# Two cross-attention layers on one core: keys, queries and row maxima in two f32r parts on 64-row halves of the array, instead of three bf16 parts on one

## The chip, the cores and the metric

The kernel runs on one core of a Trainium2 chip, written by hand in a low-level language: each engine (TensorE or PE, VectorE or DVE, ScalarE or ACT, GpSimd or POOL, and SyncE or SP, which issues DMAs) gets its own list of instructions, and semaphores join them. The metric is the device time of one execution in microseconds, lower is better.

## The reference

Two layers of cross-attention over 32 batch elements. `x` is [32, 112, 320], the context [32, 375, 512]. There are 20 heads of 16 channels.

```python
q = heads(x @ Wq); k = heads(text @ Wk); v = heads(text @ Wv)       # layer 0: text = 77 rows, ip = the other 298
out = softmax(q k^T / 4) v + softmax(q k_ip^T / 4) v_ip
x = out @ Wo.T + bo + x
# layer 1: text = 371 rows, ip = the last 4
probs_t = softmax(q k_t^T / 4);  text_out = probs_t v_t
qsem = l2norm(probs_t @ text);   sem = qsem @ l2norm(ip)^T
probs_ip = softmax(q k_ip^T / 4 + 0.5 * sem) * spatial_mask
out = (text_out + probs_ip v_ip) @ W_out + b_out + x
```

## The kernel before

**The order.** `stage_order()` (L51 on) writes one list of stages (`o.add(kind, ...)`); every engine walks the same list and takes its part of each stage. So each engine works in order, and PE's order is that of the list. A buffer in PSUM is handed from stage to stage by `o.share`: a stage waits for the signal of the stage that had the buffer as many uses before as there are buffers. The banks `R0` to `R2` (`in_bank`, L56) serve all projections, transposes and the products with the Gram matrix; `ST` (three banks) and `PN` (two banks, `PV` and `NS`) hold scores, maxima and the products with the values.

**One round** (the loop over `b` in `stage_order`) handles one batch element's groups of layer 0 with the keys and queries of the next element among them (`groups0`, `ahead`), then the groups of layer 1 of the element before (`groups1`), then the maxima (`maxima`) of layer 0 of the next element and of layer 1 of this one, with the values, Gram matrix and closing steps in between (`between`).

**Keys and queries.** The projection of plain fp32 weights and context lands in an `R` bank. ACT rounds it to bf16 (`kst[:, 0]`), DVE forms the remainder (`rem`), ACT or DVE rounds that to bf16 (`kst[:, 1]`), POOL forms the third part (`kst[:, 2]`). SP writes the parts to DRAM and reads them back stacked by head: `Ks` [102, 20, 384] holds 16 rows for each of six products of parts, `Qs` [102, 20, 112] the matching ones. A product over 96 rows so gives the score in near fp32.

**Maxima** (`s_max`, L645 to L659 on PE): for each head one matmul, queries as weights, 375 keys as columns: three heads into `ST`, then two into `PN`, eight steps a layer. DVE takes the maximum of each row. The negated maxima are transposed (`m_T`), split into three bf16 parts (ACT, then POOL in `m_split`) and sent by DMA (L1352) as rows 96 on of `Qs`, where rows of ones in `Ks` stand against them.

**Scores** (L666 to L678): a group is four heads; for each of three blocks of 128 keys and each head, one matmul with the keys as weights (102 or 100 rows, 128 columns) and 112 query columns, 12 in a group, into the three banks of `ST`. ACT takes the exponential. `pv0` and `pv1` multiply by the values (L679 to L740, weights of 17 or 21 columns, so four matmuls stand in four column tiles), `y` (L708 to L723) multiplies `pr`, the f32r-rounded probabilities, by the Gram matrix in three results j = 0, 1, 2 with 2, 4 and 6 matmuls, each in an `R` bank that DVE frees (`w<-R,w`, L803).

Of the kernel before, what the change touches and what calls it, by code (L numbers as in the profile page):

```python
# [16 lines left out]
QPART = [0, 1, 2, 0, 1, 0]  # L17
KPART = [0, 0, 0, 1, 1, 2]
CT = [(0, 128), (128, 128), (256, 64)]
HALVES = [(0, 12), (12, 20)]  # L20
# [30 lines left out]
def stage_order():  # L51
# [4 lines left out]
    def in_bank(what, signal, value):  # L56
        o.share("R", 3, what, signal, value)

# [6 lines left out]
    def keys(b, l, m):  # L65
        o.add("k", b, l, m)
        in_bank(("k", b, l, m), "k_rem", o.at("k", b, l, m))
        o.share("rem", 2, ("k", b, l, m), "k_low", o.at("k", b, l, m))

    def queries(b, l):  # L70
        o.add("q", b, l)
        in_bank(("q", b, l), "q_rem", o.at("q", b, l))
# [54 lines left out]
    def maxima(b, l, between):  # L127
        for h in range(0, H, 5):
            for h0, wide in ((h, True), (h + 3, False)):
                o.add("s_max", b, l, h0, wide)  # L130
                if wide:
                    o.share("ST", 1, ("s_max", b, l, h0), "s_max_read", o.at("s_max", b, l, h0, wide))
                else:
                    for part in ("PV", "NS"):
                        o.share(part, 1, ("s_max", b, l, h0), "s_max_read", o.at("s_max", b, l, h0, wide))
                between()
        return m_rows(b, l)

    def m_rows(b, l):
        o.add("m_neg", b, l)  # L140
        yield
        o.add("m_T", b, l)
        in_bank(("m_T", b, l), "m_hi", o.at("m_T", b, l))
        yield
        o.add("m_split", b, l)
# [98 lines left out]
    for m in range(3):  # L244
        in_bank(("image_keys", m), "kip_rem", m + 1)
# [36 lines left out]
    for b in range(B + 1):  # L282
# [92 lines left out]
def xattn_two_layers(nc, a, out):  # L375
# [3 lines left out]
    with ctx:  # L379
# [6 lines left out]
        def sem(name):  # L386
            return ctx.enter_context(nc.semaphore(name))

        kd = [nc.dram_tensor(f"k_split{l}", [B, 3, C, T], bf16, kind="Internal").ap() for l in range(2)]
        qd = [nc.dram_tensor(f"q_split{l}", [B, 3, C, S], bf16, kind="Internal").ap() for l in range(2)]  # L390
# [10 lines left out]
        Ks = [sb(f"Ks{i}", [102, H, KW], bf16) for i in range(2)]  # L401
        Qs = [sb(f"Qs{i}", [102, H, S], bf16) for i in range(2)]
        kst = [sb(f"kst{i}", [128, 3, T], bf16) for i in range(2)]
        rem = [sb(f"rem{i}", [128, T]) for i in range(2)]
        qst = sb("qst", [128, 3, 3, S], bf16)
        qrem = sb("qrem", [128, 3, S])
# [21 lines left out]
        mrem = sb("mrem", [2 * H, S])  # L428
        ms = sb("ms", [2 * H, 3, S], bf16)
# [10 lines left out]
        kip = sb("kip", [128, 3, 3, NI], bf16)  # L440
# [37 lines left out]
        kip_mm, kip_hi, kip_rem, kip_mid, kip_low = (sem(n) for n in ("kip_mm", "kip_hi", "kip_rem", "kip_mid", "kip_low"))  # L478
# [971 lines left out]
```

## Time and profile before

| | |
|---|---|
| median of 3 runs | 2875.29 us (2874.62 to 2877.16) |
| the profiled execution | 2872.28 us, its span 2870.5 us |
| TensorE clock granted | 0.988 of full speed over the span |
| PE, DVE, ACT, POOL busy | 2730.6, 1707.2, 1252.8, 467.4 us |
| DMA | 236.31 MB, 450078 packets |

A row of the timeline is: start in us, length in us, engine, line, instruction, out<-in, shapes (for PE: rows*columns of the weights, then rows x columns that stream), type, count, and in brackets the idle time before it and what ended it. Rows of equal instructions are merged: the length then runs from the first's start to the last's end. A matmul's length holds its way through the array, so the distance between starts tells what one costs in a stream. PEld is the load of weights. An fp32 matmul appears as two passes, one of f32r as one (its type also reads f32).

### The profile page before, as it was taken

How to read it: one execution, taken by the hardware profiler on the slowest of the kernel's cores; microseconds unless marked ns; L12 is line 12 of the kernel's file. 1: busy time of each engine (PE TensorE's matmuls, PEld its weight loads, DVE VectorE, ACT ScalarE, POOL GpSimd, SP SyncE). 2: the span in 40 equal slices, each digit the busy share in tenths (PEclk: the TensorE clock that was granted, in tenths of full speed). 3: DMA queues.
4: the chain of work that ended last, by engine and by line, in shares of the span. 5: the costliest groups of instructions: out<-in, count | busy, mean ns of one | idle time of the engine just before them, and what ended most of it. 6: DMA issues, size and time to landing. Idle time of an engine off the chain costs nothing.

```text
span 2870.5 us, 61414 instructions
## 1 busy us (share of the span) xinstructions
PE 2730.6 (95%) x25096; PEld 2106.1 (73%) x25096; DVE 1707.2 (59%) x3464; ACT 1252.8 (44%) x2265; POOL 467.4 (16%) x681
## 2 busy tenths in 40 slices
PE   6899999999999999999999999999999999999977
PEld 5677777777777777777777777777777777777755
DVE  3465566655566755666655666655666655666644
ACT  2344444444444444444444444444444444444443
POOL 1111111111121111121111111111111111111100
PEclk8999999999999999999999999999999999999988
DMA  7666456765546765546664556664556654557630
GB/s 192 95 83 91 75 81 80 87 83 83 82 77 81 90 83 79 82 75 86 89 85 76 81 77 86 81 94 76 80 78 87 81 92 74 81 81 83 83 34 6
DMA packets 450078, 236.31 MB, mean 82 GB/s; under 512 B 220459, under 2 KB 449787, under 8 KB 449788
## 3 DMA queue, kind: packets, MB, share of 16 engines
q1 hardware_dynamic: 433958, 209.34, 55.0%
q10 hardware_dynamic: 15840, 23.04, 2.7%
q8 instruction: 199, 3.26, 0.6%
q14 instruction: 81, 0.66, 0.1%
HBM read 166.38 MB, written 64.59 MB: 80 GB/s over the span
## 4 chain that ended last, share of the span: by engine, by line
PE 75%; DVE 12%; SPq 4%; DMA 3%; ACT 3%; issue 2%; POOL 0%; DVEq 0%; ACTq 0%; POOLq 0%
PE R L717 7%; PE ST L674 6%; PE R L617 6%; PE R L570 5%; PE PN L691 5%; PE PN L747 5%; PE R L560 4%; PE PN L734 4%; DVE m L901 4%; PE R L566 3%; PE R L720 3%; PE R L722 3%; PE R L631 2%; PE R L632 2%; PE R L768 2%
## 5 line engine op out<-in xcount | busy, mean ns | idle before, releaser
L1135 ACT ACTIVATE p<-ST 128x1344 f32<-128x1344 f32 x320 | 413.0, 1291 | 158.6 <-PE ST L677 157.0
L717 PE MATMUL R<-pr,Gh 128*128 128x448 f32 (+1 forms) x960 | 369.0, 384 | 28.3 <-DVE acc L803 28.3
L806 DVE SCALAR_TENSOR_TENSOR w<-p,pr 128x1344 f32<-128x1344 f32 x160 | 249.3, 1558 | 227.0 <-ACT pr L1150 227.0
L803 DVE TENSOR_TENSOR rem<-R,kst 128x375 f32<-128x375 f32 (+1 forms) x160 | 87.5, 547 | 484.9 <-ACT kst L1030 484.9
L803 DVE TENSOR_TENSOR w<-R,w 128x448 f32<-128x448 f32 (+1 forms) x480 | 290.7, 622 | 105.0 <-PE R L722 96.7
L631 PE MATMUL R<-wvh,ch 128*128 128x320 f32 (+3 forms) x896 | 302.5, 338 | 11.2 <-DVE cl L803 10.9
L632 PE MATMUL R<-wvh,cl 128*128 128x320 f32 (+3 forms) x896 | 279.6, 312 | 0.0
L674 PEld LDWEIGHTS ST<-Qs,Ks 100*128 100x128 bf16 (+1 forms) x3520 | 186.9, 98 | 91.9 <-issue 33.0
L1196 POOL TENSOR_TENSOR kst<-rem,kst 128x375 bf16<-128x375 f32 (+1 forms) x160 | 146.2, 914 | 618.4 <-ACT kst L1030 319.8
L674 PE MATMUL ST<-Qs,Ks 100*128 100x112 bf16 (+1 forms) x3520 | 229.4, 214 | 15.6 <-DMA Qs<-ms 6.7
L1150 ACT ACTIVATE pr<-ST 128x1344 fp32r<-128x1344 f32 x160 | 205.3, 1283 | 81.0 <-PE R L722 81.0
L717 PEld LDWEIGHTS R<-pr,Gh 128*128 128x128 f32 (+1 forms) x960 | 176.5, 184 | 78.6 <-DVE acc L803 39.6
L634 PE MATMUL R<-wvl,ch 128*128 128x320 f32 (+3 forms) x672 | 209.6, 312 | 0.0
L1196 POOL TENSOR_TENSOR cl<-cT,ch 128x476 fp32r<-128x476 f32 x126 | 156.7, 1244 | 297.8 <-ACT ch L1030 297.8
L1030 ACT ACTIVATE V<-R 128x320 f32<-128x320 f32 (+2 forms) x160 | 70.3, 440 | 287.6 <-PE R L635 287.6
L1030 ACT ACTIVATE kst<-R 128x375 bf16<-128x375 f32 (+1 forms) x160 | 77.5, 484 | 253.3 <-PE R L572 138.8
L905 DVE TENSOR_REDUCE m<-ST 112x3 f32<-112x1113 f32 x128 | 167.9, 1312 | 24.3 <-PE ST L658 21.1
L1196 POOL TENSOR_TENSOR qst<-qrem,qst 128x336 bf16<-128x336 f32 x64 | 54.2, 847 | 783.2 <-DVE qst L892 783.2
L1030 ACT ACTIVATE pvt<-PN 128x112 f32<-128x112 f32 (+1 forms) x320 | 97.4, 304 | 187.6 <-PE PN L738 128.9
L720 PE MATMUL R<-pr,Gl 128*115 128x448 f32 (+1 forms) x480 | 176.2, 367 | 0.0
L722 PE MATMUL R<-pr,Gl 128*128 128x448 f32 (+1 forms) x480 | 176.0, 367 | 0.0
L631 PEld LDWEIGHTS R<-wvh,ch 128*128 128x128 f32 (+3 forms) x896 | 162.8, 182 | 17.5 <-issue 11.8
(178 smaller groups left out, 5833.1 us busy)
## 6 DMA issues: line engine op xcount, KB each, us to landing
Ks<-k_split SPq DMA_DIRECT2D x384, 140.6 KB, 6.5
k_split<-kst SPq DMA_DIRECT2D x128, 281.2 KB, 3.0
Ks<-k_split SPq DMA_DIRECT2D x384, 93.8 KB, 9.6
Qs<-q_split SPq DMA_DIRECT2D x384, 70.0 KB, 9.4
cT<-in_ctxT ACTq DMA_DIRECT2D x30, 750.0 KB, 4.7
q_split<-qst SPq DMA_DIRECT2D x128, 84.0 KB, 2.0
k_split<-kst SPq DMA_DIRECT2D x64, 140.6 KB, 2.8
xT<-in_xT SPq DMA_DIRECT2D x32, 192.0 KB, 3.2
```

What stands on the lines that cost most here:

```text
L631: e.matmul(r[0:n, 0:C], h[:, k, 0:n], wh[:, k, :], start=k == 0, stop=False)
L632: e.matmul(r[0:n, 0:C], lo[:, k, 0:n], wh[:, k, :], start=False, stop=False)
L634: e.matmul(r[0:n, 0:C], h[:, k, 0:n], wl[:, k, :], start=False, stop=False)
L674: e.matmul(ST[:, u, S * h:S * h + S], Ks[l][0:m, GH * g + h, 128 * u:128 * u + 128], Qs[l][0:m, GH * g + h, :], start=True, stop=True)
L717: e.matmul(r[0:nj, 0:QW], Gh[0:ROWS[u], q:q + nj], pr[0:ROWS[u], QW * u:QW * u + QW], start=u == 0, stop=False)
L720: e.matmul(r[0:nj, 0:QW], Gl[0:ROWS[u], q:q + nj], pr[0:ROWS[u], QW * u:QW * u + QW], start=False, stop=False)
L722: e.matmul(r[0:nj, 0:QW], Gl[0:nj, GO[j]:GO[j] + nj], pr[0:nj, QW * j:QW * j + QW], start=False, stop=True).then_inc(y_mm, 1)
L803: return e.tensor_tensor(to, x, y, op)
L806: return e.scalar_tensor_tensor(out=to, in0=x, scalar=s, in1=y, op0=op0, op1=op1)
L1030: return e.activation(to, x, ACT.Copy, scale=scale)
L1135: e.activation(p32[i][:].rearrange("p (u q) -> p u q", u=3), st, ACT.Exp).then_inc(p_whole, 1)
L1196: return e.tensor_tensor(to, x, y, ALU.subtract)
```

## The change

1. Keys, queries and negated maxima are kept as two f32r parts (rounded value, and one DVE subtraction). `Ks`, `Qs`, `kst`, `qst`, `ms`, `kip` are f32r; `rem`, `qrem`, `mrem` and the casts and POOL subtractions go. A head takes 3 x 16 rows (high*high, high*low, low*high) instead of 6 x 16.
2. Even heads lie in rows 0 to 47 (plus 4 or 3 rows for maxima), odd heads in rows 64 to 111 (plus the same). Two heads are issued one behind the other, one for each half; the halves write to different banks.
3. `ST` has four banks (`s` = half), the `R` banks are two. The maxima go in seven steps a layer: four, two, four, two, four, two and two heads.
4. The Qs rows of the maxima are sent in 8 (layer 0) and 4 (layer 1) DMAs instead of 6 and 3. Stacks of keys and queries keep six DMAs each.
5. The last four matmuls of each `pv` signal instead of the last one; ACT waits for both halves; `ORDER` maps heads to their places in p.

```diff
-QPART = [0, 1, 2, 0, 1, 0]
-KPART = [0, 0, 0, 1, 1, 2]
+QPART = [0, 0, 1]
+KPART = [0, 1, 0]
+KR, HALF = 3 * D, 64
+HP = H // 2
+ORDER = [0, 2, 1, 3]
+MAX_STEPS = [(0, 2, True), (2, 1, False), (3, 2, True), (5, 1, False), (6, 2, True), (8, 1, False), (9, 1, True)]
...
-        o.share("R", 3, what, signal, value)
+        o.share("R", 2, what, signal, value)
...
-        in_bank(("k", b, l, m), "k_rem", o.at("k", b, l, m))
-        o.share("rem", 2, ("k", b, l, m), "k_low", o.at("k", b, l, m))
+        in_bank(("k", b, l, m), "k_low", o.at("k", b, l, m))
...
-        Ks = [sb(f"Ks{i}", [102, H, KW], bf16) for i in range(2)]
-        Qs = [sb(f"Qs{i}", [102, H, S], bf16) for i in range(2)]
+        Ks = [sb(f"Ks{i}", [128, HP, KW], f32r) for i in range(2)]
+        Qs = [sb(f"Qs{i}", [128, HP, S], f32r) for i in range(2)]
...
-        ST = pb("ST", [128, 3, 512])
+        ST = pb("ST", [128, 4, 512])
...
-        R = [pb(f"R{i}", [128, 512]) for i in range(3)]
+        R = [pb(f"R{i}", [128, 512]) for i in range(2)]
...
+        def head_rows(x, pair, n, half):
+            return x[HALF * half:HALF * half + n, pair]
...
                 elif kind == "s_max":
...
-                    for u in range(n - 1):
-                        e.matmul(to[0:S, u, 0:T], Qs[l][0:96, h0 + u, :], Ks[l][0:96, h0 + u, 0:T], start=True, stop=True)
+                    for j in range(n):
+                        for half in range(2):
+                            to = ST[0:S, 2 * half + j, 0:T + 1] if wide else PN[0:S, half, 0:T + 1]
+                            mm = e.matmul(to, head_rows(Qs[l], p0 + j, KR, half), head_rows(Ks[l], p0 + j, KR, half)[:, 0:T + 1],
+                                          start=True, stop=True)
...
                 elif kind == "scores":
...
-                        for h in range(GH):
-                            if u < 2 or h < GH - 1:
-                                e.matmul(ST[:, u, S * h:S * h + S], Ks[l][0:m, GH * g + h, 128 * u:128 * u + 128],
-                                         Qs[l][0:m, GH * g + h, :], start=True, stop=True)
+                        for j in range(2):
+                            for half in range(2):
+                                to = ST[:, 2 * half + u // 2, 256 * (u % 2) + S * j:256 * (u % 2) + S * j + S]
+                                mm = e.matmul(to, head_rows(Ks[l], 2 * g + j, m, half)[:, 128 * u:128 * u + 128],
+                                              head_rows(Qs[l], 2 * g + j, m, half), start=True, stop=True)
...
                 elif kind == "k":
...
-                    tt(rm[:, 0:n], r[:, 0:n], s[:, 0, 0:n], ALU.subtract).then_inc(k_rem, 1)
-                    if j % 2:
-                        w.wait_ge(k_rem, j + 1)
-                        e.tensor_copy(s[:, 1, 0:n], rm[:, 0:n]).then_inc(k_mid, 1)
+                    tt(s[:, 1, 0:n], r[:, 0:n], s[:, 0, 0:n].bitcast(fp32), ALU.subtract).then_inc(k_low, 1)
...
+                elif kind == "m_T":
...
+                    tt(ms[0:n, 1, :], R[slot["R", ("m_T", b, l)]][0:n, 0:S], ms[0:n, 0, :].bitcast(fp32),
+                       ALU.subtract).then_inc(m_low, 1)
...
+                elif kind == "m_out":
...
-                        for u in range(3):
-                            r0 = 96 + 3 * c + u
-                            e.dma_start(Qs[l][r0:r0 + 1, :, :], ms[H * c:H * c + H, u, :]).then_inc(d_m[l], 16)
+                        for half in range(2):
+                            r0, h0 = HALF * half + KR + 2 * c, H * c + HP * half
+                            for u in range(2):
+                                e.dma_start(Qs[l][r0 + u:r0 + u + 1].bitcast(fp32),
+                                            ms[h0:h0 + HP, u, :].bitcast(fp32)).then_inc(d_m[l], 16)
```

How PE's order changes in the stretch of the maxima, around the product with the image values (`vbd`) and the second block of the Gram matrix (`cT`), before:

```order
L656 MATMUL ST<-Ks,Qs 112x375 [waits s_max_read]
L656 MATMUL ST<-Ks,Qs 112x375
L658 MATMUL ST<-Ks,Qs 112x375
L797 MATMUL R<-vbd,prT 112x320 [waits vbd_made,ip_T_copied,g_lo]
L656 MATMUL PN<-Ks,Qs 112x375 [waits s_max_read]
L658 MATMUL PN<-Ks,Qs 112x375
L642 MATMUL R<-cT 128x247 x3
L643 MATMUL R<-cT 128x247
```

and after:

```order
L656 MATMUL PN<-Ks,Qs 112x376 [waits s_max_read]
L656 MATMUL PN<-Ks,Qs 112x376
L793 MATMUL R<-vbd,prT 112x320 [waits vbd_made,ip_T_copied]
L656 MATMUL ST<-Ks,Qs 112x376 [waits s_max_read]
L656 MATMUL ST<-Ks,Qs 112x376
L644 MATMUL R<-cT 128x247 [waits v_copied]
L644 MATMUL R<-cT 128x247 x2
L645 MATMUL R<-cT 128x247
```

The maxima steps still stand singly between full-height stages; a step is one or two pairs, and each matmul has 48 rows in one half.

On PE, the first group of `y` in a round (`Gh`, `Gl` are the parts of the Gram matrix; `pvT_read` is DVE's reading of the transposed products with the values, `w_times_y` its reading of a `y` result), before:

```order
L674 MATMUL ST<-Qs,Ks 128x112 [waits p_round]
L674 MATMUL ST<-Qs,Ks 128x112 x10
L677 MATMUL ST<-Qs,Ks 128x112
L717 MATMUL R<-pr,Gh 128x448 [waits v_copied]
L722 MATMUL R<-pr,Gl 128x448
L717 MATMUL R<-pr,Gh 128x448 [waits v_copied]
L720 MATMUL R<-pr,Gl 128x448
L717 MATMUL R<-pr,Gh 128x448
L722 MATMUL R<-pr,Gl 128x448
L717 MATMUL R<-pr,Gh 115x448 [waits pvT_read]
```

and after:

```order
L676 MATMUL ST<-Qs,Ks 128x112 [waits p_round]
L676 MATMUL ST<-Qs,Ks 128x112 x11
L716 MATMUL R<-pr,Gh 128x448 [waits v_copied]
L721 MATMUL R<-pr,Gl 128x448
L716 MATMUL R<-pr,Gh 128x448 [waits pvT_read]
L719 MATMUL R<-pr,Gl 128x448
L716 MATMUL R<-pr,Gh 128x448
L721 MATMUL R<-pr,Gl 128x448
L716 MATMUL R<-pr,Gh 115x448 [waits w_times_y]
```

The wait for `pvT_read` moved from the third result to the second, and the third now waits for the reader of the first.

On SP, around the rows of the maxima, before:

```order
L1308 DMA xn<-in_x 112x320
L1363 DMA out<-x_1 112x320
L1352 DMA Qs<-ms 1x20x112 x6
L1303 DMA xT<-in_xT 128x3x128
L1317 DMA k_split<-kst 128x3x375
L1352 DMA Qs<-ms 1x20x112 x3
```

and after:

```order
L1280 DMA xn<-in_x 112x320
L1340 DMA out<-x_1 112x320
L1328 DMA Qs<-ms 1x10x112 x8
L1275 DMA xT<-in_xT 128x3x128
L1289 DMA k_split<-kst 128x2x375
L1328 DMA Qs<-ms 1x10x112 x4
```

The place of the rows in SP's queue stays, behind the store of an output; there are more of them, with half the heads each.

## Rows read from the trace of the kernel before

**Rows 1.** The page: busy time by engine, and the chain by engine.
```profile
PE 2730.6 (95%) x25096; PEld 2106.1 (73%) x25096; DVE 1707.2 (59%) x3464; ACT 1252.8 (44%) x2265; POOL 467.4 (16%) x681
...
PE 75%; DVE 12%; SPq 4%; DMA 3%; ACT 3%; issue 2%; POOL 0%; DVEq 0%; ACTq 0%; POOLq 0%
```

**Rows 2.** Windows of one round: stretch, length, busy us of each engine.
```profile
1497.50:1523.30 25.80, 24.25 (x139) 19.32 (x138) 23.74 (x56) 9.99 (x28) 6.79 (x8) 1.00 0.50 84
1523.30:1549.30 26.00, 25.91 (x311) 19.78 (x311) 7.41 (x16) 12.11 (x21) 5.87 (x10) 1.00 0.19 53
1549.30:1584.50 35.20, 34.26 (x339) 26.01 (x334) 22.24 (x39) 16.98 (x25) 1.93 (x3) 1.00 0.90 98
sum 87.00, PE 84.41 PEld 65.11 DVE 53.39 ACT 39.08 POOL 14.59; mean PE 28.14 PEld 21.70 DVE 17.80 ACT 13.03 POOL 4.86
```

**Rows 3.** Waits of PE, the longest: us in total, times, longest.
```profile
PE R L717 <- DVE acc L803: 28.3, 30, 0.9
```

**Rows 4.** The chain in order of time, in the maxima.
```profile
1519.35 3.99 DMA Qs<-ms
```

**Rows 5.** Timeline of the maxima: DVE, SP's queue, the next scores.
```profile
1512.39 1.32 DVE L905 TENSOR_REDUCE m<-ST 112x3 f32<-112x1113 f32 x1
...
1515.12 0.32 SPq L1363 DMA_DIRECT2D out<-x  x1
...
1515.49 4.58 SPq L1352 DMA_DIRECT2D Qs<-ms  x6
...
1523.39 0.71 PE L674 MATMUL ST<-Qs,Ks 102*128 102x112 bf16 x11 [0.28 <-DMA Qs<-ms]
```

**Rows 6.** Timeline of PE: a scores group and what follows.
```profile
1527.00 0.71 PE L674 MATMUL ST<-Qs,Ks 102*128 102x112 bf16 x11
...
1527.60 1.12 PE L566 MATMUL R<-cT,wk 128*128 128x128 f32 x8
```

**Rows 7.** Timeline of PE: a step of the maxima.
```profile
1507.84 0.30 PE L635 MATMUL R<-wvl,ch 128*128 128x320 f32 x1
1507.98 0.48 PE L656 MATMUL ST<-Ks,Qs 96*112 96x375 bf16 x2
...
1508.46 0.70 PE L797 MATMUL R<-vbd,prT 80*112 80x320 f32 x2
```

**Rows 8.** Timeline of PE: f32r value matmuls behind a step of the maxima.
```profile
1506.08 0.45 PE L631 MATMUL R<-wvh,ch 128*128 128x320 f32 x1
1506.36 0.32 PE L632 MATMUL R<-wvh,cl 128*128 128x320 f32 x1
```

**Rows 9.** Timeline of PE in narrow windows: the query projection's passes.
```profile
1541.68 0.28 PE L617 MATMUL R<-xT,wq 128*128 128x128 f32 x1
...
1541.89 0.37 PE L617 MATMUL R<-xT,wq 64*128 64x128 f32 x1
...
1542.10 0.27 PE L617 MATMUL R<-xT,wq 64*128 64x128 f32 x1
...
1542.30 0.38 PE L617 MATMUL R<-xT,wq 128*128 128x128 f32 x1
...
1542.52 0.39 PE L617 MATMUL R<-xT,wq 128*128 128x128 f32 x2
...
1542.74 0.28 PE L617 MATMUL R<-xT,wq 128*128 128x128 f32 x1
```

**Rows 10.** Timeline of PE, narrow window: values, four column tiles.
```profile
1544.62 0.28 PE L691 MATMUL PN<-p,V 128*17 128x112 f32 x4
```

**Rows 11.** Timeline of the first and last y group of a round.
```profile
1554.75 0.37 PE L717 MATMUL R<-pr,Gh 128*128 128x448 f32 x1
...
1556.67 0.46 PE L717 MATMUL R<-pr,Gh 128*115 128x448 f32 x1 [0.94 <-DVE acc L803]
...
1580.66 0.36 PE L717 MATMUL R<-pr,Gh 128*115 128x448 f32 x1
1580.77 1.16 DVE L803 TENSOR_TENSOR w<-R,w 128x448 f32<-128x448 f32 x2
```

More of the change, by code:

```diff
@@ L127, in maxima @@
     def maxima(b, l, between):
[L128 to L136, printed above, removed]
+        for p0, n, wide in MAX_STEPS:
+            o.add("s_max", b, l, p0, n, wide)
+            for part in ("ST",) if wide else ("PV", "NS"):
+                o.share(part, 1, ("s_max", b, l, p0), "s_max_read", o.at("s_max", b, l, p0, n, wide))
+            between()
         return m_rows(b, l)
@@ L387, in sem @@
             return ctx.enter_context(nc.semaphore(name))
-        kd = [nc.dram_tensor(f"k_split{l}", [B, 3, C, T], bf16, kind="Internal").ap() for l in range(2)]
-        qd = [nc.dram_tensor(f"q_split{l}", [B, 3, C, S], bf16, kind="Internal").ap() for l in range(2)]
+        kd = [nc.dram_tensor(f"k_split{l}", [B, 2, C, T], fp32, kind="Internal").ap() for l in range(2)]
+        qd = [nc.dram_tensor(f"q_split{l}", [B, 2, C, S], fp32, kind="Internal").ap() for l in range(2)]
+        rowsd = [nc.dram_tensor(f"rows{i}", shape, fp32, kind="Internal").ap()
+                 for i, shape in enumerate(([4, HP, KW], [3, HP, KW], [1, HP, S]))]
         vipd = nc.dram_tensor("v_ip", [B * NIP, C], fp32, kind="Internal").ap()
@@ L400, in xattn_two_layers @@
         wo = [sb(f"wo{i}", [128, 3, C]) for i in range(2)]
-        Ks = [sb(f"Ks{i}", [102, H, KW], bf16) for i in range(2)]
-        Qs = [sb(f"Qs{i}", [102, H, S], bf16) for i in range(2)]
[L403 to L406, printed above, removed]
+        Ks = [sb(f"Ks{i}", [128, HP, KW], f32r) for i in range(2)]
+        Qs = [sb(f"Qs{i}", [128, HP, S], f32r) for i in range(2)]
+        kst = [sb(f"kst{i}", [128, 2, T], f32r) for i in range(2)]
+        qst = sb("qst", [128, 3, 2, S], f32r)
         V0t = sb("V0t", [TEXT0, H, FV0])
@@ L427, in xattn_two_layers @@
         mn = sb("mn", [S, 2 * H])
-        mrem = sb("mrem", [2 * H, S])
-        ms = sb("ms", [2 * H, 3, S], bf16)
+        ms = sb("ms", [2 * H, 2, S], f32r)
         sip = [sb(f"sip{i}", [S, H, NIP]) for i in range(2)]
@@ L439, in xattn_two_layers @@
         vbd = sb("vbd", [H * NIP, C])
-        kip = sb("kip", [128, 3, 3, NI], bf16)
+        kip = sb("kip", [128, 3, 2, NI], f32r)
         ninv = sb("ninv", [128, B, NIP])
@@ L539, in v_place, with by_pair @@
             return (V0 if l == 0 else V1)[0:n, t], n
-        k_odd = {}
-        for key, j in nk.items():
-            k_odd[key] = sum(1 for i in nk.values() if i <= j and i % 2 == j % 2)
+        def head_rows(x, pair, n, half):
+            return x[HALF * half:HALF * half + n, pair]
+        def by_pair(x):
+            return x.rearrange("p (j s) n -> p s j n", s=2)
         def tensor(e):
@@ L782, in tensor @@
                     w.wait_ge(ns_read, b + 1)
[L783 to L784 removed]
+                    for h, i in enumerate(ORDER[:-1]):
+                        e.transpose(r[0:S, 96 * h:96 * h + 96], nss[:, S * i:S * i + S], ident[0:96, 0:96])
                     e.transpose(r[0:S, 288:384], nss[:, 336:448], ident[0:96, 0:96]).then_inc(ns_T, 1)
@@ L1325, in sync @@
                         w.wait_ge(s_mm, s_nth[b - 1, l, 2 if part == 0 else 4])
-                    for g in range(6):
-                        e.dma_start(Ks[l][D * g:D * g + D, h0:h1, 0:T],
-                                    kd[l][b, KPART[g], D * h0:D * h1, :].rearrange("(h d) t -> d h t", d=D)).then_inc(
-                                        d_kr[l][part], 16)
+                    for half in range(2):
+                        for i in range(3):
+                            r0 = HALF * half + D * i
+                            heads = kd[l][b, KPART[i]].rearrange("(j s d) t -> s d j t", s=2, d=D)[half, :, h0:h1, :]
+                            e.dma_start(Ks[l][r0:r0 + D, h0:h1, 0:T].bitcast(fp32), heads).then_inc(d_kr[l][part], 16)
                 elif kind == "q":
```

237 lines of the change are left out of this document (102 added, 135 removed).

## The prediction

> **What bounds the kernel now.** I read the page first: the matrix engine's share and the chain that ended last [rows 1]. PE is busy 95% of the span and carries 75% of the chain, so PE's stream of matmuls is the bound and everything else matters where PE waits for it. Then the busy time of each engine in the three stretches of one round (one batch element) [rows 2]: the stretch of the maxima (25.8 us) has PE 24.25 and DVE 23.74 us busy, the stretch of layer 0's groups (26.0 us) has PE 25.91 and DVE 7.41, the stretch of layer 1's groups (35.2 us) PE 34.26 and DVE 22.24. A round is 87 us and there are 32. So outside the maxima only PE's own time counts; in the maxima two engines are nearly full. Third, the list of waits: the longest of PE's, for DVE before a y group, is 28.3 us in all [rows 3]. What the change removes from DVE, ACT and POOL in the key and query chains (the remainders, casts and second subtractions) therefore buys next to nothing: it lies beside a PE that does not wait for it. Fourth, the chain in the stretch of the maxima: its last piece is not PE but the DMA of the maxima rows, 3.99 us [rows 4], and before it the six issues of that DMA on SP, 4.58 us, which start at 1515.49 behind an output store [rows 5]. The next scores start at 1523.39, after 0.28 us of waiting for that DMA.
>
> **Scores, 12 matmuls a group, 320 groups.** Today 12 bf16 matmuls take 0.60 us (1527.00 to 1527.60), 50 ns each, and the first matmul behind them starts 0.05 us after the last: weights of 128 columns load unseen and nothing drains [rows 6]. After the change each group is 6 pairs, one matmul in each 64-row half. No row shows f32r with 112 columns, nor two row halves at once; these are the unknown prices.
> Streaming: ten f32r matmuls of 320 columns take 1.48 us (1506.36 to 1507.84 [rows 7, 8]), 148 ns each or 0.46 ns a column: 52 ns for 112 columns.
> Switch of row mode: the query projection alternates 128-row and 64-row matmuls. Steady 128-row passes are 0.11 us apart (1542.52 to 1542.74, two); across a switch the distance is 0.21 and 0.20, so about 0.095 us of draining each way; and the pass behind the switch is followed after 0.21 or 0.22 instead of 0.11 [rows 9]: the load of 128 four-byte columns, about 0.105 us, is no longer hidden. By the page TensorE: Matmul & The Clock Gate of the Trainium skill (sections LDWEIGHTS and Weight-path perf modes), a load costs its columns, not its rows, and the fast load is for dtypes narrower than fp32 only; by that rule halving the rows saves nothing and the step from bf16 to f32r makes each load dearer, and the trace agrees (hidden at 50 ns in [rows 6], 105 ns bare in [rows 9]).
> Are the two halves concurrent? The nearest row is four fp32 matmuls in four column tiles that together take 0.28 us [rows 10], where a single pass has a length of 0.27 [rows 9]; so tiles run beside each other, and I take it for row halves. The page TensorEngine Tiling (Array Packing) of the Trainium skill (Tiling Modes, Key Properties) says that different tiles can load and multiply in parallel; by that rule a pair costs what one matmul with its load costs, as forecast, and no row here shows it for row halves. The same section says that a change of tiling mode drains the array; with it the time is the forecast's too, and without it rival D's.
> A pair then costs the larger of 52 ns (stream) and about 108 ns (load, both halves loading together). I take the load, since it is the nearest row; bounds are 52 ns (load hidden) and 214 ns (the two loads one after the other; short f32r streaming no faster than the two passes of plain fp32, 2 x 0.11 x 112/128 = 0.19 us, lies between these). A group: first load 0.105, five distances of 0.108, last stream 0.052, drain 0.095: 0.79 us against 0.60, so +0.19. Behind it the next stage's load is bare, 0.105, where today it costs between nothing and 0.13 (0.28 instead of 0.148 behind a bf16 stage [rows 8]); I take +0.03. In front, five of ten groups now follow a stage without a mode of its own (keys, values, a transpose, a projection), +0.095 for half of them, +0.05. Sum +0.28 us a group, 320 groups: +90 us. With 52 ns a pair it is -0.05 a group, -16 us; with 214 ns +0.91, +291 us.
>
> **Maxima, 40 heads a round.** Today 0.16 us a head (3 in 0.48 [rows 7]). After: 20 pairs of 376 columns, 376 x 0.46 = 174 ns, the load of 112 columns hidden under it: 3.5 us instead of 6.4. But each of 14 steps is now a mode of its own in the middle of 128-row stages: drain 0.095, bare load 0.09, drain 0.095, bare load behind 0.03 more than today: 0.31 a step, about 13 separate steps, 4.0 us. PE's time rises by 1.1 us a round. The price of the halves failing to run together is 20 x 174 ns more, 3.5 us.
> What ends the stretch is the chain of the maxima rows. The m rows of layer 0 go out in eight DMAs instead of six: at 4.58/6 = 0.76 us each [rows 5] that is +1.5 us. The rounding parts now come one subtraction after the copy instead of three POOL steps, but SP stands at the output store until 1515.12 anyway, so that gain is hidden; and the store waits for a DVE addition that now stands behind a four-head reduction, 1.32/3 = 0.44 us longer [rows 5]. So +1.9 us if the issue price holds for smaller transfers (10 source rows instead of 20), and if that price halves, 8 x 0.38 = 3.05 us, the chain is shorter and PE's 1.1 us less its present idle time (25.80 - 24.25) decides: about 0. I take +1.5, nearer to the row as it stands: 31 rounds, +46 us.
>
> **Banks.** Scores take four banks, so the other results have two instead of three. A stage now waits for the reader of the stage two before. I looked where that reader is late. First y group of a round: its second result (1554.75) must now wait for the same reader, acc, that today the third waits for (1556.67, after 0.94 of waiting): the second's four matmuls, 4 x 0.205 us, are no longer in front of the wait, +0.8 us. Last y group: the third result started at 1580.66, and the reader of the first ends about 1580.77 + 0.58 = 1581.35: +0.7 us [rows 11]. Elsewhere the reader is done or so nearly (the three middle groups, where longer scores in front give DVE more room). +1.5 us a round, 32 rounds: +48 us. Bounds: 0.7 (only one of the two) and 3 us (all results of the y groups late by as much again), 22 to 96 us.
>
> **Sum.** 2872.28 us for the profiled execution (span 2870.5) + 90 + 46 + 48 = 3056 us; the median of the runs is 2875.29, 3 us more, which I add in part: 3058 us, 6.4% slower.
>
> **Rivals.**
> A: the two halves' loads go one after the other (or short f32r streams slower): pair 190 to 214 ns. For it: nothing shows parallel loads of rows. Against: the four tiles of [rows 10] start together. Scores cost +240 to +290 instead of +90: 3210 to 3260 us.
> B: the halves do not run together at all. Scores as in A, maxima 3.5 us more a round, +110: about 3370 us. Against it is [rows 10].
> C: loads are fully hidden, the drains stay: scores -16, the rest as forecast: 2950 us.
> D, on the other side of before: f32r halves load hidden under each other and no drain separates them from the 128-row stages. A group is then 6 x 52 = 0.31 us instead of 0.60, -0.29, 320 groups: -93 us. The maxima cannot give much, since DVE is busy 23.74 of 25.8 us and the chain runs through it: about -0.5 us a round, -15; banks +22. 2786 us. The mechanism decides from the point where a switch costs less than 0.05 us; [rows 9] show 0.2 for each, twice in a row, with plain fp32, which is what speaks against it. What speaks for it: the matrix engine is the bound, and the change halves the number of streams there.
> E: all cancels, within 0.2% (about 6 us, what a measurement here can tell from no change).
>
> **Chances.** Forecast with its own bounds (2990 to 3130) 0.51; A 0.17; B 0.05; C 0.11; D 0.14; E 0.02. Faster by over 0.2%: 0.14; within: 0.02; slower: 0.84. The range takes in C and A and leaves out D and B: 2890 to 3270.
>
> **What would show it.** In the profile after: in a scores group, pairs that start together (within some 10 ns) and are about 108 ns apart; 52 would be C or D, 190 or more A, and starts evenly spaced without pairs B. A distance of about 0.2 us from the last matmul before a maxima step to its first, and again behind it; 0.05 would be D. 14 stretches of maxima with PE about 7.5 us in a round against 6.4. PE waiting before a y group's second result, for acc, and in the last y group before its third, for w. SP's issues of the maxima rows: eight, 6.1 us, and scores of layer 0 waiting for that DMA by more than 0.28 us. DVE, ACT and POOL less busy without an effect on the span. The forecast is wrong if the mode switch costs PE nothing, or if the loads of the two halves queue up.

## The result and the profile after

The changed kernel takes 3131.66 us (median of 4 runs, 3120.56 to 3135.34) against 2876.22 us (4 runs, 2874.62 to 2878.33) of the kernel before on the same chip: ratio 1.0881, 95% interval 1.0853 to 1.0910, 255 us slower. The forecast was 3058 us, the range 2890 to 3270. The profiled execution is the longest of the four: 3135.34 us, its span 3133.5 us. The mean granted TensorE clock fell from 0.988 to 0.960.

The page of the kernel after: busy time by engine, granted clock in 40 slices, shares of the chain.

```profile
PE 2940.5 (94%) x25096; PEld 2135.2 (68%) x25096; DVE 1619.3 (52%) x3250; ACT 1214.7 (39%) x2121; POOL 202.2 (6%) x265
...
PEclk8999999999999999999999999999999999999988
...
PE 67%; DVE 14%; SPq 7%; issue 4%; ACT 4%; DMA 4%; DVEq 0%; POOL 0%; ACTq 0%; POOLq 0%
```

Against [rows 1]: PE has as many instructions and is busy 210 us longer, DVE, ACT and POOL are busy 88, 38 and 265 us less, and the span does not gain by it. The other 53 us of the span's 263 are time in which PE stands. On the chain PE's share fell by 8 points, and SP's queue rose from 4 to 7%.

Windows of one round of the kernel after, cut at the first maxima, the first scores of layer 0 and the first scores of layer 1; columns as in [rows 2], the number behind POOL is the granted clock.

```profile
1630.30:1659.60 29.30, 26.93 (x142) 18.82 (x141) 23.62 (x55) 10.59 (x27) 4.96 (x4) 0.94 0.22 47
1659.60:1686.85 27.25, 27.22 (x311) 20.57 (x311) 5.55 (x13) 10.88 (x16) 0.39 (x3) 1.00 0.24 74
1686.85:1726.25 39.40, 37.37 (x336) 27.22 (x331) 21.02 (x34) 16.28 (x24) 0.98 (x2) 0.96 0.78 112
```

The middle stretch has the full clock, and PE does not wait in it: 27.25 against 25.95 us for five scores groups. The other two contain something that [rows 2] do not: a clock below 1.00.

One round is a sample of one. So I cut the traces at the same three places in the 23 to 28 rounds between 300 and 2700 us (mid-run, below). Us of each stretch, the median, and the shortest in brackets where a fall of the clock makes it differ:

| kernel | maxima | layer 0 | layer 1 | sum of the medians |
|---|---|---|---|---|
| before | 25.91 | 25.95 | 34.70 | 86.6 |
| after | 28.99 (27.31) | 27.25 | 39.43 (37.89) | 95.7 |
| b_two_banks | 26.03 | 25.95 | 37.34 | 89.3 |
| b_reordered | 25.90 | 25.95 | 33.94 | 85.8 |
| b_two_banks_reordered | 26.01 | 25.95 | 36.97 | 88.9 |
| a_first_move | 27.50 | 27.25 | 37.37 | 92.1 |
| a_bf16_halves | 28.05 (26.99) | 25.21 | 37.01 | 90.3 |
| a_one_half | 29.04 | 30.58 | 42.09 (40.56) | 101.7 |
| a_reordered | 30.03 (28.37) | 27.25 | 37.36 | 94.6 |

The list of waits, PE's longest, kernel after (us in all, times, longest):

```profile
PE R L716 <- DVE acc L799: 42.1, 30, 1.4
PE R L786 <- DVE fus L799: 40.9, 31, 4.1
PE ST L676 <- DMA Qs<-ms: 27.2, 32, 5.4
PE R L716 <- DVE w L799: 20.3, 33, 0.6
```

Before, acc had 28.3 us [rows 3], fus 19.7 and the maxima rows 6.7, and w was not in the list. The timeline of the kernel after: PE at a step of the maxima, SP's queue at the maxima rows, and the first two scores groups on PE (of the second first its first two matmuls alone, from a narrow window, then all twelve):

```profile
1633.47 0.31 PE L637 MATMUL R<-wvl,ch 128*128 128x320 f32 x1
1633.70 0.60 PE L656 MATMUL ST<-Ks,Qs 48*112 48x376 f32 x4
1634.23 0.58 PE L644 MATMUL R<-cT 128*128 128x375 f32 x1
...
1651.04 6.84 SPq L1328 DMA_DIRECT2D Qs<-ms  x8
...
1659.63 0.88 PE L676 MATMUL ST<-Qs,Ks 52*128 52x112 f32 x12 [0.92 <-DMA Qs<-ms]
...
1663.55 0.32 PE L676 MATMUL ST<-Qs,Ks 52*128 52x112 f32 x2
...
1663.55 0.88 PE L676 MATMUL ST<-Qs,Ks 52*128 52x112 f32 x12
1664.36 0.49 PE L568 MATMUL R<-cT,wk 128*128 128x128 f32 x2
```

In the second group the first two matmuls together take 0.32 us, hardly more than a single one (0.28 on the mean): they start at once, the halves are a pair. In 85% of all pairs the partners start 0 to 4 ns apart, and pairs stand 110 ns apart; the group takes 0.81 us to the next matmul (forecast 0.79) against 0.60 [rows 6]. A step of the maxima starts 0.23 us behind the last value matmul, which alone would be 0.148: the switch of row mode is paid. The issues of the eight DMAs take 6.84 us on SP in this round, which is one of the longest; the median of 24 rounds in mid-run is 6.13 us, 0.77 each (0.76 was expected). The scores wait 0.92 us for these DMAs here and 0.67 in the median, against 0.03 in the median before.

What the forecast does not have, kernel after, two falls of the granted clock: windows of 3.4 us before and behind the point, twice (columns as above).

```profile
1594.60:1598.00 3.40, 2.49 (x22) 1.86 (x21) 2.59 (x4) 2.56 (x3) 0.00 (x0) 1.00 1.12 128
1598.00:1601.40 3.40, 2.91 (x8) 2.52 (x9) 1.79 (x5) 0.00 (x0) 0.00 (x0) 0.61 1.14 132
1635.90:1639.30 3.40, 2.19 (x11) 0.94 (x9) 3.30 (x10) 2.02 (x8) 1.27 (x1) 1.00 0.00 0
1639.30:1642.70 3.40, 3.40 (x16) 3.06 (x14) 2.26 (x3) 0.42 (x2) 1.21 (x1) 0.56 0.00 0
```

And the same two places in the timeline of PE:

```profile
1596.73 0.36 PE L721 MATMUL R<-pr,Gl 128*128 128x448 f32 x1
1598.49 0.56 PE L716 MATMUL R<-pr,Gh 128*128 128x448 f32 x1 [1.40 <-DVE acc L799]
1598.86 0.57 PE L719 MATMUL R<-pr,Gl 128*128 128x448 f32 x1
...
1638.59 0.26 PE L786 MATMUL R<-ident_sb,fus 112*80 112x112 f32 x1 [1.21 <-DVE fus L799]
...
1639.97 0.47 PE L633 MATMUL R<-wvh,ch 128*128 128x320 f32 x1
1640.24 0.47 PE L634 MATMUL R<-wvh,cl 128*128 128x320 f32 x1
```

Behind an idle time of 1.40 us, matmuls of 448 columns are 0.37 us apart instead of 0.205, behind one of 1.21 us those of 320 columns 0.27 instead of 0.148. The granted clock is then at the lower of its two levels, 1.2 instead of 2.4 GHz, for about 3.4 us. Rounds with such a stretch take 1.5 us (layer 1) and 1.6 us (maxima) more in the median than rounds without. In the trace of before it is there for 70.6 us in 7 pieces, all at the start and the end; in the trace after for 250.0 us in 53 pieces, 44 of them (160 us) in the middle. Before has no idle time of PE above 0.95 us in mid-run.

### The profile page after: what moved, and what is told of

The parts are those of the page before. It is cut to its first block, busy times and chain, and to the rows that moved or that the text cites. A ratio compares the mean times of both kernels' runs of the same rounds, so it can differ in the third digit from the quotient of the medians.

```text
span 3133.5 us, 61223 instructions
## 1 busy us (share of the span) xinstructions
PE 2940.5 (94%) x25096; PEld 2135.2 (68%) x25096; DVE 1619.3 (52%) x3250; ACT 1214.7 (39%) x2121; POOL 202.2 (6%) x265
## 4 chain that ended last, share of the span: by engine, by line
PE 67%; DVE 14%; SPq 7%; issue 4%; ACT 4%; DMA 4%; DVEq 0%; POOL 0%; ACTq 0%; POOLq 0%
PE ST L676 8%; PE R L716 7%; PE R L619 5%; SPq L1328 5%; PE PN L692 5%; PE R L572 4%; PE R L562 4%; DVE m L886 3%; PE PN L743 3%; PE R L719 3%; DVE w L802 3%; PE R L568 3%; PE PN L733 3%; DMA Qs<-ms 3%; PE R L721 3%
## 5 line engine op out<-in xcount | busy, mean ns | idle before, releaser
L716 PE MATMUL R<-pr,Gh 128*128 128x448 f32 (+1 forms) x960 | 405.5, 422 | 62.4 <-DVE acc L799 42.1
L799 DVE TENSOR_TENSOR kst<-R,kst 128x375 fp32r<-128x375 f32 (+1 forms) x160 | 87.6, 548 | 504.2 <-ACT kst L1022 504.2
L676 PEld LDWEIGHTS ST<-Qs,Ks 52*128 52x128 f32 (+1 forms) x3840 | 248.7, 190 | 124.2 <-issue 55.0
L676 PE MATMUL ST<-Qs,Ks 52*128 52x112 f32 (+1 forms) x3840 | 291.9, 282 | 33.7 <-DMA Qs<-ms 27.2
L716 PEld LDWEIGHTS R<-pr,Gh 128*128 128x128 f32 (+1 forms) x960 | 186.9, 195 | 164.3 <-DVE acc L799 53.3
L890 DVE TENSOR_REDUCE m<-ST 112x4 f32<-112x1484 f32 (+1 forms) x128 | 192.5, 1504 | 10.8 <-PE ST L656 6.7
L719 PE MATMUL R<-pr,Gl 128*115 128x448 f32 (+1 forms) x480 | 188.6, 393 | 0.0
L1022 ACT ACTIVATE kst<-R 128x375 fp32r<-128x375 f32 (+1 forms) x160 | 77.2, 482 | 284.0 <-PE R L574 156.1
L634 PEld LDWEIGHTS R<-wvh,cl 128*128 128x128 f32 (+3 forms) x896 | 171.1, 191 | 0.3
L572 PE MATMUL R<-cT,wk 128*128 128x298 f32 x576 | 162.1, 418 | 0.0
```

The costliest lines, as they stand in the source:

```text
L572: e.matmul(r[:, TEXT0:T], wk[1][:, k, c0:c0 + 128], c[:, k, TEXT0:T], start=k == 0, stop=False, skip_group_check=True)
L634: e.matmul(r[0:n, 0:C], lo[:, k, 0:n], wh[:, k, :], start=False, stop=False)
L676: mm = e.matmul(to, head_rows(Ks[l], 2 * g + j, m, half)[:, 128 * u:128 * u + 128], head_rows(Qs[l], 2 * g + j, m, half), start=True, stop ...
L716: e.matmul(r[0:nj, 0:QW], Gh[0:ROWS[u], q:q + nj], pr[0:ROWS[u], QW * u:QW * u + QW], start=u == 0, stop=False)
L719: e.matmul(r[0:nj, 0:QW], Gl[0:ROWS[u], q:q + nj], pr[0:ROWS[u], QW * u:QW * u + QW], start=False, stop=False)
L799: return e.tensor_tensor(to, x, y, op)
```

## The experiments

Names with b_ are edits of the kernel before, with a_ of the kernel after. Ratios are against the kernel before, run beside it on the same chip.

| kernel | median us | ratio (95%) | clock | at half clock, us (pieces) |
|---|---|---|---|---|
| b_two_banks | 2979.61 | 1.0361 (1.0344 to 1.0378) | 0.981 | 112.7 (20) |
| b_max_64rows | 2946.82 | 1.0248 (1.0233 to 1.0264) | 0.987 | 77.3 (8) |
| b_scores_64rows | 2918.29 | 1.0155 (1.0136 to 1.0174) | 0.985 | 88.4 (7) |
| a_bf16_halves | 2974.90 | 1.0346 (1.0330 to 1.0362) | 0.978 | 134.4 (29) |
| a_one_half | 3346.95 | 1.1640 (1.1611 to 1.1669) | 0.972 | 187.1 (28) |
| a_stream_56 | 3127.56 | 1.0882 (1.0853 to 1.0911) | 0.956 | 276.6 (56) |
| a_reordered | 3125.73 | 1.0871 (1.0846 to 1.0896) | 0.966 | 212.0 (32) |
| a_bf16_reordered | 3015.17 | 1.0488 (1.0467 to 1.0509) | 0.974 | 159.4 (32) |
| a_first_move | 3049.89 | 1.0608 (1.0584 to 1.0631) | 0.982 | 113.4 (12) |
| b_reordered | 2853.71 | 0.9924 (0.9904 to 0.9944) | 0.987 | 74.3 (8) |
| b_two_banks_reordered | 2945.43 | 1.0248 (1.0229 to 1.0268) | 0.989 | 68.1 (7) |
| b_reordered_ip_later | 2855.95 | 0.9938 (0.9917 to 0.9959) | 0.988 | 69.9 (8) |

### Do the two halves run together? a_one_half

The odd heads' matmuls read the even heads' rows (rows 0 to 47), so the odd heads are left out of the maxima and the scores.

```diff
-            return x[HALF * half:HALF * half + n, pair]
+            return x[0:n, pair]
```

> The changed kernel with both heads of a pair read from the lower 64 rows (so the even head is computed twice, the odd one left out): same instructions, but no two halves at once. Theory that halves run together: each scores pair goes from 0.11 to about 0.22 us (two loads one behind the other in one half), +0.65 us a group, 320 groups +208 us; maxima 20 x 0.174 us more a round, of which idle time hides up to 1, +80 to +108 us: about 3420 us. Rival (the halves never ran together, the pair distance is issue alone): within 20 us of 3131.

3346.95 us, 215 more than after and 73 less than expected. A scores group of this kernel, timeline of PE:

```profile
1605.16 1.54 PE L676 MATMUL ST<-Qs,Ks 51*128 51x112 f32 x12
1606.63 0.47 PE L716 MATMUL R<-pr,Gh 128*128 128x448 f32 x1
```

1.47 us instead of 0.81: the 12 start one after the other, 0.11 us apart in the median, as far as pairs do in the kernel after. Layer 0 with its five groups takes 3.33 us more, 0.67 a group, as expected. The maxima take only 1.4 us more (29.04 against 27.60 in rounds of the kernel after without a fall), where about 3 were expected. Forecast and rival B are told apart: in the kernel after, the halves load and multiply beside each other, and where they are kept from it the time comes near to rival B's 3370. That is what the page TensorEngine Tiling (Array Packing) of the Trainium skill (Key Properties) says of different tiles, and the trace agrees for row halves with the 110 ns a pair.

### What bounds a pair, the load or the stream? a_stream_56 and a_bf16_halves

a_stream_56: each scores matmul streams 56 of its 112 query columns; the other half of the scores is left out (`ST` is set to zero once, at the start).

```diff
-  to = ST[:, 2 * half + u // 2, 256 * (u % 2) + S * j:256 * (u % 2) + S * j + S]
+  to = ST[:, 2 * half + u // 2, 256 * (u % 2) + S * j:256 * (u % 2) + S * j + S // 2]
-                head_rows(Qs[l], 2 * g + j, m, half), start=True, stop=True)
+                head_rows(Qs[l], 2 * g + j, m, half)[:, 0:S // 2], start=True, stop=True)
```

> The changed kernel, but each scores matmul streams only the first 56 of 112 query columns (the other half of the scores is left out). Theory that a pair is bound by the load of its weights, 128 f32r columns, 0.11 us: pairs stay 0.11 us apart, only the last stream of a group is shorter by 0.03 us, 320 groups -8 us: about 3123 us. Rival that f32r streams few columns slowly (0.11 us for 112): pairs at 0.06 us, -0.27 us a group, about 3045 us.

a_bf16_halves: the same layout in bf16. Keys, queries and maxima then hold two parts of bf16, 16 bits where the kernel before has three parts and 24.

```diff
-        Ks = [sb(f"Ks{i}", [128, HP, KW], f32r) for i in range(2)]
-        Qs = [sb(f"Qs{i}", [128, HP, S], f32r) for i in range(2)]
+        Ks = [sb(f"Ks{i}", [128, HP, KW], bf16) for i in range(2)]
+        Qs = [sb(f"Qs{i}", [128, HP, S], bf16) for i in range(2)]
...
```

> The changed kernel with its two parts in bf16 instead of f32r (layout, halves, banks and order kept; the parts hold fewer bits). Theory that f32r loads of 128 columns at 0.11 us set the pairs: a pair falls from 0.11 to about 0.05 us, a scores group from 0.81 to about 0.42, 320 groups -122 us, and 0.07 us less a maxima step, -30: about 2980 us, if the waits and clock falls stay. Rival that draining and pairing are the price: hardly under 3080 us, with pairs still about 0.1 us apart.

Half the stream: 3127.56 us, 4 less than after, the intervals on top of each other. Half the width of the loaded type: 2974.90 us, 157 less. The groups of the two, timeline of PE, first with 56 columns, then in bf16:

```profile
1603.54 0.85 PE L676 MATMUL ST<-Qs,Ks 51*128 51x56 f32 x12
1604.33 0.48 PE L716 MATMUL R<-pr,Gh 128*128 128x448 f32 x1
```

```profile
1607.54 0.47 PE L676 MATMUL ST<-Qs,Ks 51*128 51x112 bf16 x12
1608.00 0.47 PE L716 MATMUL R<-pr,Gh 128*128 128x448 f32 x1
```

0.79 us with half the columns, 0.46 in bf16 with all of them (0.40 in the median of all groups, pairs 0.05 us apart), 0.81 after. So the stream does not set the pair and the width of the type does: that fits the load of 128 four-byte columns, as forecast from [rows 9]. A floor of 0.11 us for a pair of f32r matmuls, whatever they load, would fit as well; no run varies the columns of the weights. The rule in the page TensorE: Matmul & The Clock Gate of the Trainium skill (Weight-path perf modes), no fast load for fp32, agrees, if f32r counts as fp32 there, which the page does not say. The bf16 group is also shorter than the 0.60 us of before [rows 6]: 64-row halves do pay where the load is hidden, and in layer 0 as a whole, drains included, they save 0.74 us (25.21 against 25.95). What is left of a_bf16_halves above before, 100 us, is maxima, banks and clock.

### What does a switch of row mode cost? b_scores_64rows and b_max_64rows

In the kernel before the scores' matmuls (first edit) or those of the maxima (second edit) read 64 rows; the terms in the other rows are left out. The count of matmuls, their columns and the banks stay; only the row mode (128 rows of the array or 64) changes.

```diff
-                    m = 102 if l == 0 else 100
+                    m = 64
```

```diff
-  e.matmul(to[0:S, u, 0:T], Qs[l][0:96, h0 + u, :], Ks[l][0:96, h0 + u, 0:T], start=True, stop=True)
+  e.matmul(to[0:S, u, 0:T], Qs[l][0:64, h0 + u, :], Ks[l][0:64, h0 + u, 0:T], start=True, stop=True)
```

> The kernel before, but the scores' bf16 matmuls read 64 rows of 102 or 100 (they leave out two products of parts and the maxima). My step: draining behind each of 320 groups 0.095 us plus 0.03 of bare load, and 0.095 in front of half of them: 0.17 to 0.19 us a group, +55 to +62 us, about 2935 us. Rival (changes of mode are cheap): within 10 us of before.

> The kernel before, but the maxima's bf16 matmuls read 64 of the 96 rows (they leave out two of the six products of parts), so each of their steps is a change of row mode. My step: 0.095 us of draining in, 0.095 out, and the next load bare: about 0.24 us for each of 12.6 separate steps, 3.1 us of PE a round, of which DVE and the maxima rows' DMA hide about 0.5: about +80 us, 2955 us. Rival (the change of mode costs little and the f32r loads are the price): under +20 us.

+44 us for 320 groups, 0.14 us each. The group itself keeps its length (eleven matmuls in 0.71 us, as in [rows 6]), timeline of PE:

```profile
1507.10 0.71 PE L674 MATMUL ST<-Qs,Ks 64*128 64x112 bf16 x11
...
1507.66 0.21 PE L677 MATMUL ST<-Qs,Ks 64*128 64x112 bf16 x1
```

It is the entry and the exit that cost: from the first matmul of a group to the first one behind it the median over all groups is 0.69 us against 0.59 before, so 0.10 for the exit. For the maxima +72 us, 2.0 us a round in the stretch of the maxima (27.92 against 25.91), with 16 steps. So the price exists, rival D (no drain) is excluded, and it is somewhat below what [rows 9] gave: 44 us where 55 to 62 were expected, 72 where 80 were.

### What do two banks cost? b_two_banks and b_two_banks_reordered

```diff
-        o.share("R", 3, what, signal, value)
+        o.share("R", 2, what, signal, value)
-        R = [pb(f"R{i}", [128, 512]) for i in range(3)]
+        R = [pb(f"R{i}", [128, 512]) for i in range(2)]
```

> The kernel before with two R banks instead of three, nothing else. My step on banks: +1.5 us a round where PE waits for acc in the first y group and for w in the last, 32 rounds, so about 2924 us. Rival: the waits also bring falls of the granted clock, as in the changed kernel (250 us at half clock there, 71 before), then 2950 to 2990 us and a mean clock under 0.98. If the banks are harmless: within 10 us of before.

+105 us, twice the 48 of the forecast. The table by stretch puts all of it in layer 1 (37.34 against 34.70; the other two differ by 0.12 at most), where the y groups are. PE's waits in the kernel with two banks, and the timeline of PE in its first y group:

```profile
PE R L717 <- DVE acc L803: 52.4, 30, 1.8
PE R L717 <- DVE w L803: 20.4, 33, 0.6
```

```profile
1615.80 0.47 PE L717 MATMUL R<-pr,Gh 128*128 128x448 f32 x1 [1.74 <-DVE acc L803]
...
1617.18 0.57 PE L720 MATMUL R<-pr,Gl 128*115 128x448 f32 x1
1617.55 0.57 PE L717 MATMUL R<-pr,Gh 128*115 128x448 f32 x1
```

The wait for acc is 24 us longer in all, 0.8 a round, and the one for w is new, 0.6 a round: these are the 0.8 and 0.7 of the forecast. To them come a fall of the clock behind the wait in some rounds (42 us more at half clock, so up to 21 us of time), and something in the three middle y groups, which the forecast held to be free. The kernel after shows it, timeline of PE in a middle group, the third result begins at 1608.02:

```profile
1607.75 0.36 PE L721 MATMUL R<-pr,Gl 128*128 128x448 f32 x1
1608.02 0.46 PE L716 MATMUL R<-pr,Gh 128*115 128x448 f32 x1
1608.32 0.36 PE L719 MATMUL R<-pr,Gl 128*115 128x448 f32 x1
1608.52 0.36 PE L716 MATMUL R<-pr,Gh 128*115 128x448 f32 x1
```

Distances 0.27 and 0.30 where 0.205 is the pace: 0.16 us lost, though no wait is listed. The load of the weights is what waits for the bank: DVE's reading ends at 1607.97, the load starts at 1608.02 together with its matmul, where those in front of it start 0.2 us ahead of theirs. From the first to the last start of a y group the mean is 2.57 us before and 3.15 with two banks: 0.58 x 160 groups = 93 us of the 105. By position in the round, in the median without a fall, the five groups take 0.83, 0.16, 0.42, 0.33 and 0.88 us longer than before. So the three middle ones make 0.9 of the 2.6 us a round.

b_two_banks_reordered has the same two banks and the move of the next section:

> The kernel before with two R banks and the transposed products moved ahead (no wait for acc). Theory that half of the bank price (+105 us measured) is this wait, 52 us, with the clock falls behind it (42 us more at half clock, 21 lost), and the rest the y groups' third results: 2895 to 2915 us, clock back at 0.987. Rival (two banks cost wherever they are reused): above 2950 us.

2945.43 us where 2895 to 2915 were expected, 92 above the same kernel with three banks (b_reordered, 2853.71), without a fall in mid-run. So two banks cost some 90 us by themselves, and the clock is only part of the 105.

### Is it the wait for acc that pulls the clock down? a_first_move, a_reordered, b_reordered

The move: in the first group of layer 1, PE takes the transposes of the last products (`pvT`, two matmuls) ahead of the values matmuls and not behind them. DVE then reads their bank (acc) before its 1.56 us multiplication and the two parts of the context, behind which that reading stands in the kernel before, timeline of DVE:

```profile
1553.55 1.56 DVE L806 SCALAR_TENSOR_TENSOR w<-p,pr 128x1344 f32<-128x1344 f32 x1 [2.71 <-ACT pr L1150]
...
1556.33 0.29 DVE L803 TENSOR_TENSOR acc<-R,rz 112x128 f32<-112x128 f32 x1
```

```diff
         def among1(g, end):
+            if g or not end:
+                take(first, 1)
             if g == 0 and b + 1 < B:
                 take(pieces, 1)
-            if end or g:
-                take(first, 1)
```

> The changed kernel with only the first move (transposed products ahead; the order in the maxima as in the changed kernel). The move in the maxima had traded one wait for others. Theory: the wait for acc (42 us) and one of two clock falls a round (about 90 us at half clock, 45 lost) go: 3040 to 3070 us. Rival (any order has as many waits): 3110 or more, as with both moves.

3049.89 us, 82 less than after. acc is gone from PE's waits (the list of this kernel); w has risen from 20.3 to 46.9 us, 0.9 us at the longest:

```profile
PE R L716 <- DVE w L799: 46.9, 63, 0.9
PE R L786 <- DVE fus L799: 40.7, 31, 4.1
```

Layer 1 takes 37.37 us against 39.43 (37.89 in rounds of the kernel after in which the clock stays up). Of the 2.06 us a round 1.5 are the fall, 0.5 the shorter wait. Half-clock time goes from 250.0 to 113.4 us. One thing I cannot explain: the stretch of the maxima also lost its fall in all but 2 of 25 rounds (27.50 against 28.99), where the kernel after has one in 18 of 24, though its wait for fus stayed as it was.

The length of the wait does not decide. In b_two_banks PE waits 1.74 us in every round of mid-run, and the clock falls behind it in 9 of 25. In a_one_half it falls in layer 1 in 15 of 23 rounds, and the idle time in front of it is 0.73 us, less than the 0.94 that before has at full clock. Windows before and behind such a fall, and PE at that place:

```profile
1605.60:1609.00 3.40, 2.67 (x17) 2.11 (x17) 3.07 (x7) 1.29 (x1) 0.00 (x0) 1.00 1.12 129
1609.00:1612.40 3.40, 3.40 (x24) 2.61 (x27) 1.25 (x2) 0.45 (x3) 0.00 (x0) 0.50 1.12 141
```

```profile
1608.04 0.47 PE L716 MATMUL R<-pr,Gh 128*128 128x448 f32 x1 [0.73 <-DVE acc L799]
```

What decides between rounds and kernels stays open.

a_reordered has a second move besides, to take fus's wait away too (the pieces of `finish1` at other counts in `between`):

```diff
-            if count[0] in (1, 2, 3, 4, 6, 8, 9):
+            if count[0] in (1, 2, 3, 5, 7, 9, 10):
```

> The changed kernel with two stages moved in the list: the transposed products of layer 0's last part ahead of the values and of DVE's w of the first y group, and the image-weights transpose one place later. It keeps every matmul. Theory that the clock falls (250 us at half speed, 125 us lost, against 71 and 35 before) follow PE's two longest waits, 1.4 us for acc and 1.2 us for fus: both waits go (42 + 41 us), and with them most of the clock falls (about 85 us): 2950 to 2990 us, clock 0.98 or more. Rival that the clock falls come from half-height matmuls: the waits go but the clock stays at 0.96, about 3070 us.

3125.73 us: the second move costs 76 of the 82 again. In PE's waits fus fell to 16.3 us, and three others took its place:

```profile
PE ST L656 <- DVE sip L891: 40.2, 32, 1.6
PE R L666 <- DVE mn L900: 19.6, 32, 1.5
PE ST L656 <- DVE m L886: 16.5, 62, 1.4
```

The stretch of the maxima is 30.03 us: the wait for sip is 1.26 us in the mean (40.2 us in 32), and the falls are back (in 19 of 24 rounds, up to 6.8 us long). 2950 to 2990 us had been expected. The same pair of moves with the bf16 halves:

> Halves with bf16 parts (fewer bits) and both moves. If the moves take about 130 us from the f32r kernel, here it has 54 + 44 us of waits and 64 us more at half clock than before (32 lost): 2860 to 2890 us, near the kernel before. Rival (the banks are the price, not the order): above 2930 us.

3015.17 us, 40 more than a_bf16_halves, with the same sip wait (40.3 us), and far from the 2860 to 2890 expected.

The first move alone on the kernel before:

> The kernel before with only the first of these moves: the transposed products ahead of the values and of DVE's w. The 28.3 us in which PE waits for acc should go: about 2848 us, 1% faster than before. Rival (the wait moves to the next thing DVE owes): within 6 us of before.

2853.71 us, ratio 0.9924 (0.9904 to 0.9944): faster than both kernels. PE's waits in it, of which acc is no longer one:

```profile
PE PN L656 <- DVE m L901: 19.9, 42, 0.6
PE R L790 <- DVE fus L803: 19.7, 31, 4.2
```

To take fus's wait away there too, I moved two of the pieces of `finish1` later:

```diff
-            if count[0] in (1, 2, 3, 5, 7, 9, 10):
+            if count[0] in (1, 2, 3, 6, 8, 9, 10):
```

> The kernel before with the transposed products ahead and the image-weights transpose, product and store one place later in the maxima. PE's wait for fus, 19.7 us, should go: about 2835 us. Rival (the closing steps are then later than the next stage needs them, as in the changed kernel with both moves): 2855 us or more.

2855.95 us, no change (2835 was expected): fus fell to 4.2 us, m rose to 42.9. The stretch has DVE nearly as full as PE, and a wait taken from one stage comes up at the next. It is 1.34 us long and comes in every round of mid-run, longer than the one for fus in the kernel after, and the clock stays up behind it in all of them. PE at one such place, and the windows before and behind it:

```profile
1496.69 0.37 PE L656 MATMUL PN<-Ks,Qs 96*112 96x375 bf16 x1 [1.34 <-DVE m L901]
```

```profile
1493.90:1497.30 3.40, 2.06 (x10) 1.04 (x9) 3.29 (x10) 1.11 (x5) 1.27 (x1) 1.00 1.29 129
1497.30:1500.70 3.40, 3.40 (x22) 2.93 (x21) 3.16 (x6) 1.20 (x3) 1.20 (x1) 1.00 0.10 15
```

## Why the prediction was right, and by how much it fell short

**The bound.** Right. PE is 94% busy, and DVE, ACT and POOL lost 391 us of busy time for nothing.

**Scores.** Right, and for the reason given. Forecast 0.28 us a group (its terms, 0.19, 0.03 and 0.05, add up to 0.27); measured 1.30 us for the five of layer 0, 0.26 each, in a stretch with no wait and the full clock. The stream does not set the pair (a_stream_56), the width of the loaded type does (a_bf16_halves), the halves are concurrent (a_one_half), the switch is paid (b_scores_64rows). Rivals A, B, C and D are each excluded by one of these.

**Maxima.** Right in size, and in its main term. Rounds without a fall take 27.60 us in the kernel after (median of six) and 27.48 in a_first_move (of 23) against 25.91: +1.6 to +1.7, forecast 1.5. The eight issues take 6.13 us against 4.61, the forecast's 6.1, and the scores then wait for these DMAs in every round. Two other terms were off and partly cancel: the issues begin 0.9 us later in the stretch and not 0.44, and the scores start 2.25 us behind their end instead of 3.08, which the forecast did not have. That the time lies near the 1.5 that was taken, and not near the 1.9 that the terms gave, is luck.

**Banks.** The places were right, the size was not. In the kernel after, layer 1 without a fall takes 3.2 us more, of which 1.3 are scores, if they cost there what they cost in layer 0: 1.9 for the banks against 1.5. The y groups give the same by position: 0.5 us in the first (forecast 0.8), 0.9 in the last (0.7) and 0.5 in the three middle ones (nothing). On the kernel before the same edit costs 2.6 us a round without a fall. That longer scores give DVE more room fits: the middle three cost 1.2 us a round in a_bf16_halves (a group of scores 0.40 us), 0.9 in b_two_banks (0.60) and 0.5 in the kernel after (0.81), but also 0.5 in a_one_half (1.47). The step that failed is "Elsewhere the reader is done or so nearly": nearly is not free, 0.17 us each at the least.

**The clock.** Missing from the sum altogether: this is the term that the forecast put at nothing without a reason. Without falls a round takes 6.2 us more than before (27.60 + 27.25 + 37.91 against 86.56), 31 rounds 192 us, near the forecast's 184. The falls are the rest: over all rounds the means lie 1.3 us (maxima) and 1.1 us (layer 1) above rounds without one, 31 rounds 77 us. Both together are 269 us, the span grew by 263. I had worked out that PE would stand longer before the first y group (0.94 + 0.8 = 1.7 us; measured 1.74 in b_two_banks and 1.40 in the kernel after), had seen the clock at 0.988, and did not ask what an idle time longer than any of before does to it. That the falls of layer 1 go when this wait goes is shown by a_first_move. Which waits bring a fall is not: the lengths 0.73, 1.34 and 1.74 us above say that this question alone would not have given the answer.

**The range** reached to 3270 for rival A and so held the time by luck, for a reason that was not in it. The forecast's own range (2990 to 3130) missed the median by 2 us.

## What to carry to other kernels

Before halving the rows of a short matmul, compare its stream with the load of its weights in the new type: packing two heads side by side halved the number of streams, but the pair was bound by what four-byte weights cost, which bf16 had hidden. A wait that is added to the engine that bounds the kernel can cost twice: by its own length, and by a fall of the granted clock behind it (1.5 to 1.6 us each here). Put the second into the range even where the trace before shows no fall, and do not judge by the length of the wait: here falls stood behind 0.73 us in one kernel, and none behind 1.34 us in another. And count a PSUM bank that comes free "just in time" as late.

## What the runs showed that I had not expected

- Two 64-row halves pay in bf16 (a group 0.40 us against 0.60) and lose in f32r (0.81).
- A bank freed barely late, with no wait in the list, costs 0.16 us at the next matmuls, because the load of the weights waits for it. Of the 92 us between two banks and three in the reordered kernels, the listed waits for w account for 54.
- The falls of the clock depend on more than the idle time before them: with the first of a round gone, the second mostly went too, and one and the same wait of 1.74 us brought a fall in 9 rounds of 25.
